# Attention stage of a macaron transformer block: weighing at steps 1, 5, 9 and 13, bank orders reversed between batches, a V projection two steps later, statistics one batch later

## The reference

```python
x = x + 0.5 * ffn(layernorm(x))     # x: (16, 256, 128) float32, 16 batches of 256 tokens
x = x + attn(layernorm(x))          # 16 heads of 8, softmax over 256 keys, biases
x = x + 0.5 * ffn(layernorm(x))
# ffn: silu(x W1) * (x W2) -> gelu(. H1) -> gelu(. H2) -> . W3, hidden width 512
```

## Time and profile before

| | us |
|---|---|
| median of 3 runs | 666.66 (664.96 to 670.3) |
| profiled execution | 672.58, its span 670.8 |
| attention stage, from the first `max_rows` to the first matmul of the second feed-forward phase | 225.12 to 490.85 |
| PE busy | 630.9 (94%) |
| ACT busy | 466.8 (70%) |
| DVE busy | 440.4 (66%) |

### The profile page before, as it was taken

The page is one execution under the profiler, slowest core; times in us unless marked ns, Lnnn a source line. Parts: engine busy times, 40 slices in busy tenths (PEclk is TensorE's granted clock), DMA queues, the critical chain, the costliest instruction groups (busy, mean ns, idle before and its releaser), DMA issues.

```text
span 670.8 us, 12974 instructions
## 1 busy us (share of the span) xinstructions
PE 630.9 (94%) x4452; PEld 462.1 (69%) x4452; DVE 440.4 (66%) x1036; ACT 466.8 (70%) x791; POOL 92.4 (14%) x256
## 2 busy tenths in 40 slices
PE   1969999999999799999999999999999999999996
PEld 1748878788776566666666566666567878878785
DVE  4844666858545867877878887784076485656742
ACT  2646786968864357777777868774477796887964
POOL 2601010012101012222222222102001001010000
PEclk9969999999999679999999999995689999999999
DMA  9100000000051704370715343300000001001011
GB/s 296 41 2 1 1 0 0 1 0 0 1 195 56 251 2 153 101 245 13 249 62 189 118 133 127 128 1 1 1 3 1 1 0 33 0 0 31 1 31 33
DMA packets 36674, 41.97 MB, mean 63 GB/s; under 512 B 2448, under 2 KB 27280, under 8 KB 36624
## 3 DMA queue, kind: packets, MB, share of 16 engines
q1 hardware_dynamic: 36624, 41.31, 18.2%
HBM read 22.42 MB, written 18.87 MB: 62 GB/s over the span
## 4 chain that ended last, share of the span: by engine, by line
PE 82%; DVE 7%; ACT 4%; issue 3%; DMA 2%; POOL 0%; SPq 0%; ACTq 0%; POOLq 0%
PE bank L1008 45%; PE bank L1118 10%; PE bank L1092 7%; PE bank L1105 5%; PE bank L1107 4%; DVE neg_max L816 2%; PE bank L1150 2%; PE bank L1136 2%; ACT probs L630 1%; PE bank L1081 1%; PE bank L1073 1%; PE bank L1055 1%; DVE act_lo L766 1%; PE bank L1077 1%; DMA QK<-qk_scratch 1%
## 5 line engine op out<-in xcount | busy, mean ns | idle before, releaser
L1008 PE MATMUL bank<-act_hi,WH 128*128 128x512 f32 x576 | 233.3, 405 | 6.8 <-issue 5.4
L1008 PE MATMUL bank<-act_lo,WH 128*128 128x512 f32 x576 | 228.8, 397 | 0.0
L816 DVE TENSOR_REDUCE neg_max<-bank 128x2 f32<-128x512 f32 x256 | 166.9, 682 | 50.0 <-PE bank L1092 46.8
L630 ACT ACTIVATE probs<-bank 128x512 f32<-128x512 f32 x256 | 140.8, 597 | 54.6 <-PE bank L1107 52.5
L786 DVE TENSOR_TENSOR act_lo<-full,act_hi 128x512 fp32r<-128x512 f32 x128 | 88.0, 689 | 124.2 <-ACT act_hi L529 124.1
L527 ACT ACTIVATE full<-bank,SG 128x512 f32<-128x512 f32 x128 | 88.0, 687 | 69.1 <-PE bank L1008 68.7
L1008 PEld LDWEIGHTS bank<-act_hi,WH 128*128 128x128 f32 x576 | 109.1, 189 | 37.2 <-issue 6.0
L1008 PEld LDWEIGHTS bank<-act_lo,WH 128*128 128x128 f32 x576 | 109.1, 189 | 25.4 <-issue 0.5
L1105 PE MATMUL bank<-QK 32*128 32x256 f32 x512 | 113.0, 348 | 3.5 <-ACT probs L630 1.8
L1107 PE MATMUL bank<-m_parts,SEL 32*128 32x256 f32 x512 | 96.0, 293 | 0.0
L1092 PE MATMUL bank<-QK 32*128 32x256 f32 x512 | 83.1, 340 | 6.7 <-DVE neg_max L816 4.8
(11 more groups left out here) (91 smaller groups left out, 597.2 us busy)
## 6 DMA issues: line engine op xcount, KB each, us to landing
qk_scratch<-qk SPq DMA_DIRECT2D x64, 256.0 KB, 2.6
QK<-qk_scratch SPq DMA_DIRECT2D x16, 1024.0 KB, 7.2
X<-x SPq DMA_DIRECT2D x4, 512.0 KB, 6.9
raw_rest<-w_ffn SPq DMA_DIRECT2D x4, 512.0 KB, 6.1
out<-X SPq DMA_DIRECT2D x4, 512.0 KB, 3.2
raw<-w_ffn SPq DMA_DIRECT2D x3, 256.0 KB, 4.4
WA<-w_att SPq DMA_DIRECT2D x1, 256.0 KB, 5.2
xT<-sel SPq DMA_DIRECT2D x1, 256.0 KB, 5.1
```

The costliest lines, as they stand in the source:

```text
L630: A.activation(probs[:, v % 8, :], bank[B_BANKS[v]][:, :], ACT.Exp, scale=SCALE)\
L816: D.tensor_reduce(neg_max[:, bb, qt, n0:n0 + 2], bank[banks[u]][:, :].rearrange("p (h k) -> p h k", h=2), axis=AX.X, op=ALU.max, negate=Tr ...
L1008: ins = MM(dst, a, b, start=k == 0, stop=k == len(todo) - 1)
```

## The change

- PE weighs where v % 4 == 1, from v = 5 on: behind steps 9 and 13 of the batch and steps 1 and 5 of the next one. `in_step` ends two units earlier, and ACT's `evacuate_o` moves from step 7 to step 5.
- Even batches take the banks in the order 0, 1, 5 (and 2, 3, 7), odd batches in the order 5, 1, 0 (and 7, 3, 2). Unit 0 finds its bank used two units back, unit 1 four back, every other unit three back.
- `project_v` and ACT's `set_v` move from step 7 to step 9. `transpose_att` stays at step 7, now with no weighing ahead of it.
- The statistics of the second feed-forward phase move from batch 14 (steps 7 to 11) to batch 15 (steps 2 to 6), its normalisation from step 3 to step 10 of batch 15; POOL takes `max_again` of batch 15 before the Newton steps.

```diff
-A_BANKS = (0, 1, 5) * 4 + (0, 1, 5, 1)
-B_BANKS = (2, 3, 7) * 4 + (2, 3, 7, 3)
+A_BANKS = ((0, 1, 5) * 5 + (0,), (5, 1, 0) * 5 + (5,))
+B_BANKS = ((2, 3, 7) * 5 + (2,), (7, 3, 2) * 5 + (7,))
...
-            return [(d, v) for d, v in at if 0 <= v < UNITS + 4]
+            return [(d, v) for d, v in at if 0 <= v < UNITS + 2]
+
+        def used_last(banks, prev, u):
+            before = prev + banks[:u]
+            return next((d for d in range(1, len(before) + 1) if before[-d] == banks[u]), u + 1)
...
+            max_again(NBATCH - 1, 1)
             rsqrt_steps(NORMS1, K * NORMS1)
-            max_again(NBATCH - 1, 1)
...
-                        if v == UNITS + 3:
+                        if v == UNITS + 1:
                             evacuate_o(b - d)
...
-                    if u == 7 and v_pair is not None:
+                    if u == 9 and v_pair is not None:
                         set_v(*v_pair)
...
-                elif not more:
-                    steps, norm = norm_steps(NORMS1, 0, biased=4), (NORMS1, 0, 8)
...
-                attend(2 * i + 1, 1, prev2=not first, more=more, norm=norm)
+                if more:
+                    attend(2 * i + 1, 1, prev2=not first, norm=norm)
+                else:
+                    attend(2 * i + 1, 1, more=False, steps=norm_steps(NORMS1, 0, biased=4), steps_at=2,
+                           norm=(NORMS1, 0, 8), norm_at=10)
...
-                ahead = next(d for d in range(1, UNITS) if banks[u - d] == banks[u])
-                wait(pe, max_done, UNITS * b + u - ahead + 1)
+                wait(pe, max_done, UNITS * b + u - used_last(banks, prev, u) + 1)
...
-                last = next(d for d in range(1, UNITS) if B_BANKS[v - d] == B_BANKS[v])
-                wait(pe, exp_done, UNITS * b + v - last + 1 + CREDIT)
+                wait(pe, exp_done, UNITS * b + v - used_last(B_BANKS[bb], B_BANKS[1 - bb], v) + 1 + CREDIT)
...
-                        if v >= 7 and v % 4 == 3:
+                        if v >= 5 and v % 4 == 1:
                             weigh(*at, v // 4 - 1, 0)
                             weigh(*at, v // 4 - 1, 1)
...
-                    if u == 7 and v_pair is not None:
+                    if u == 9 and v_pair is not None:
```

More of the change, by code:

```diff
@@ L624, in _, with exp_unit @@
             ffn_phase(0)
-            def exp_unit(b, v):
+            def exp_unit(b, bb, v):
                 act.wait_ge(b_mm, UNITS * b + v + 1)
                 act.wait_ge(pv_mm, GROUPS * b + v // 4 - 2 + 1 + CREDIT)
-                A.activation(probs[:, v % 8, :], bank[B_BANKS[v]][:, :], ACT.Exp, scale=SCALE)\
+                A.activation(probs[:, v % 8, :], bank[B_BANKS[bb][v]][:, :], ACT.Exp, scale=SCALE)\
                     .then_inc(exp_done, 1)
@@ L644, in o_to_sbuf, with attend @@
                 A.activation(onT[:, :], bank[6][:, 0:SEQ], ACT.Copy).then_inc(on_T_sb, 1)
-            def attend(b, prev=True, prev2=True, own=True, steps=UNITS, ahead=None, v_pair=None):
+            def attend(b, bb, prev=True, prev2=True, own=True, steps=UNITS, ahead=None, v_pair=None):
                 for u in range(steps):
@@ L651, in attend @@
                         if v < UNITS:
-                            exp_unit(b - d, v)
-                        if v == UNITS + 3:
+                            exp_unit(b - d, (bb + d) % 2, v)
+                        if v == UNITS + 1:
                             evacuate_o(b - d)
@@ L672, in att_body @@
             def att_body(i, par, ahead=True, more=True, first=False):
-                attend(2 * i, prev=not first, prev2=not first, v_pair=(i + 1, 1 - par) if more else None)
-                attend(2 * i + 1, prev2=not first, ahead=i + 2 if ahead else None)
+                attend(2 * i, 0, prev=not first, prev2=not first, v_pair=(i + 1, 1 - par) if more else None)
+                attend(2 * i + 1, 1, prev2=not first, ahead=i + 2 if ahead else None)
             att_body(0, 0, first=True)
@@ L682, in _ @@
             att_body(NPAIR - 1, 1, ahead=False, more=False)
-            attend(NBATCH, own=False, steps=SKEW + 4)
+            attend(NBATCH, 0, own=False, steps=SKEW + 4)
             ffn_phase(1)
@@ L810, in set_bias, with max_unit @@
                 D.tensor_tensor(BO[:, :], bank[3][:, 0:P], BO[:, :], op=ALU.add).then_inc(bias_set, 1)
-            def max_unit(b, bb, u, banks=A_BANKS):
+            def max_unit(b, bb, u, banks=None):
                 dve.wait_ge(a_mm, UNITS * b + u + 1)
@@ L816, in max_unit @@
                 D.tensor_reduce(neg_max[:, bb, qt, n0:n0 + 2],
-                                bank[banks[u]][:, :].rearrange("p (h k) -> p h k", h=2), axis=AX.X,
+                                bank[(banks or A_BANKS[bb])[u]][:, :].rearrange("p (h k) -> p h k", h=2), axis=AX.X,
                                 op=ALU.max, negate=True).then_inc(max_done, 1)
@@ L944, in _, with attend @@
             ffn_phase(0)
-            def attend(b, bb, prev=True, prev2=True, more=True, steps=(), norm=None):
+            def attend(b, bb, prev=True, prev2=True, more=True, steps=(), steps_at=7, norm=None, norm_at=3):
                 for u in range(UNITS):
@@ L956, in attend @@
                         add_att(b - 2, 2 * b - 4)
-                    if u == 3 and norm is not None:
+                    if u == norm_at and norm is not None:
                         n, tile0, width = norm
@@ L961, in attend @@
                             normalise(n, tile0 + 4, 4)
-                    if u >= 7:
-                        for step in steps[u - 7:u - 6]:
+                    if u >= steps_at:
+                        for step in steps[u - steps_at:u - steps_at + 1]:
                             step()
@@ L1083, in project_v, with max_scores @@
                 ins.then_inc(v_mm, 1)
-            def max_scores(b, par, bb, u, banks=A_BANKS):
+            def max_scores(b, par, bb, u, banks, prev):
                 qt, jj, lane = a_unit(u)
                 rows = slice(32 * lane, 32 * lane + 32)
-                ahead = next(d for d in range(1, UNITS) if banks[u - d] == banks[u])
-                wait(pe, max_done, UNITS * b + u - ahead + 1)
+                wait(pe, max_done, UNITS * b + u - used_last(banks, prev, u) + 1)
                 for i in range(2):
@@ L1100, in scores @@
                 rows = slice(32 * lane, 32 * lane + 32)
-                last = next(d for d in range(1, UNITS) if B_BANKS[v - d] == B_BANKS[v])
-                wait(pe, exp_done, UNITS * b + v - last + 1 + CREDIT)
+                wait(pe, exp_done, UNITS * b + v - used_last(B_BANKS[bb], B_BANKS[1 - bb], v) + 1 + CREDIT)
                 for i in range(2):
-                    dst = bank[B_BANKS[v]][:, SEQ * i:SEQ * i + SEQ]
+                    dst = bank[B_BANKS[bb][v]][:, SEQ * i:SEQ * i + SEQ]
                     MM(dst, k_of(2 * par + bb)[rows, 2 * jj + i, P * kt:P * kt + P],
@@ L1173, in entry @@
                                 pe.wait_ge(v_set, 1)
-                            max_scores(0, 0, 0, u, ENTRY_BANKS)
+                            max_scores(0, 0, 0, u, ENTRY_BANKS, ())
                     pe.wait_ge(h_full, hl + 6)
@@ L1292, in attend @@
                     if more:
-                        max_scores(b + 1, npar, nbb, u)
+                        max_scores(b + 1, npar, nbb, u, A_BANKS[nbb], A_BANKS[bb] if prev else ENTRY_BANKS)
                     for d, v in in_step(u, prev, own):
```

## The result

| | before | after |
|---|---|---|
| median, us | 666.68 (664.96 to 670.3) | 690.06 (688.19 to 693.0) |
| ratio | | 1.0347, interval 1.0285 to 1.041 |
| profiled span | 670.8 | 691.2 |
| PE / ACT / DVE busy | 630.9 / 466.8 / 440.4 | 621.2 / 463.9 / 438.8 |

The account below looks back on a forecast made before the run. PE was taken as the bound, waiting 4.1 us per pair of batches; +11.5 (batches 2 to 11), +2.7 (12, 13), -2.45 (14) and -3 (tail) made +8.8, with the profiled execution 5.9 above the median 675.4 us, range 662 to 692.

Parts of the forecast that it names:

- The sum: PE's waits laid out by hand, plus statistics and tail: 11.5 + 2.7 - 2.45 - 3 = +8.8 us.
- changes of kind: PE blocks following another kind, 0.23 us each: 14 in an even batch instead of 16, 18 in an odd instead of 19.
- The chart of an even batch: Hand layout of PE's blocks from max_rows to the next: 16.14 us, before 15.05, +1.09.
- The waits for exponentials: Even batch, steps 9 and 13: PE waits for ACT's exponentials 2 and 6, 0.76 us twice.
- the wait for `split_max`: PE stands ahead of transpose_o from 2.07 to 2.93 us in every batch, 0.86, no longer covered by a weighing.
- Odd batches: PE waits for split_max, for add_att ahead of transpose_att, and for scale_o: 17.08 us, before 15.96, +1.12.
- The clock within the stage: Rival: waits of about 1 us bring two more stretches at 1.2 GHz, 7 us each, 689; chance 0.2.
- Batch 14: Without the eight statistics it is as batch 13, 15.05 us against 17.50: -2.45, no clock fall at step 8.
- The tail: Batch 15 and the tail, 30.9 us before: gain between 0 and 10.4 depending on the clock, taken as -3.
- the tail stays fast: Rival: batch 15 and the tail at 2.4 GHz, all of the 10.4 us instead of 3, 668; chance 0.1.
- The bank orders and V: Steps 15 and 1 lose a short wait, step 0 gains one inside scale_o's; V at step 9 costs nothing.
- The rule on changes of kind: A change of tiling mode drains TensorE; by this alone eight pairs would be 5.5 us faster.

Follow-up runs that it names:

- e3: The changed kernel with DVE's split_max ahead of maximum 2 instead of behind it: 681.15 us, ratio 1.0321 to before.
- e1: The changed kernel with the weighing, and ACT's copy of o, put back behind steps 3, 7, 11 and 15: 640.9 us, ratio 0.9685 to before.
- e9: The changed kernel with the weighing of step 1 ahead of max_rows instead of behind it: 671.5 us, ratio 1.0081 to before.
- e4: The kernel before with the late statistics alone: 663.97 us, ratio 0.9979.
- e5: The changed kernel with PE repeating the first max_scores matmul at steps 1 and 3, and step 7 of odd batches: 689.15 us, ratio 1.0305 to before.
- e10: The kernel before with the reversed bank orders of odd batches alone: 662.98 us, ratio 0.9908.
- e6: e1 with the bank orders of before; V at step 9 and late statistics stay: 651.81 us, ratio 0.976 to before.
- e7: e1 with V back at step 7, right behind the weighing there: 650.08 us, ratio 0.9721 to before.
- e2: The kernel before with only the weighing moved, behind steps 1, 5, 9, 13, and ACT's copy of o at step 5: 699.74 us, ratio 1.0584.
- e11: e1 with DVE repeating maximum 2 twice and maximum 15 once into spare cells: 666.91 us, ratio 1.0006 to before.

## Why the prediction was right and wrong

**The direction and the mechanism were right; the size was not.** The sum said that the new order costs more waits than it saves changes of kind. The chart of an even batch came out block by block. With 0 at `max_rows` of batch 4 (293.46), forecast and measured: `transpose_o` 2.93 and 2.98, `project_out` 5.00 and 5.04, weighing 7.80 and 7.78, V 8.80 and 8.78, weighing 12.05 and 11.97, next `max_rows` 16.14 and 16.20. The waits for exponentials, 0.76 twice in this chart, are booked only in part (0.19 and 0.18, ahead of them, to DVE), but the weighings behind them start when forecast. e3 shows the wait for `split_max` by itself (0.49 of it can be taken back), e1 all the waits together.

**Odd batches: 0.54 too short.** Forecast 17.08, measured 17.62. Two terms failed. One is the latency of 0.04 from an engine's end to PE's start: `add_att` ends at 316.89 and `transpose_att` starts at 317.02, 0.13; `scale_o` ends at 327.14 and `max_rows` starts at 327.28, 0.14. The other is a wait of which the chart has nothing, K's 0.17 for ACT's `qk_full`. `transpose_att` starts at 7.36 instead of 7.20, K at 11.63 instead of 11.24. The two terms make 0.36 of the 0.54; the rest is small differences. Five odd batches: 2.7 us.

**The clock within the stage: the term that was missing, some 11 us.** By e9 it is 2.4 in batch 3, 1.4 in batch 13 and 7.5 in batch 14. The forecast had it as a rival, with 7 us for each fall and 689 for two of them, at a chance of 0.2. The time is 690; that the two are so near is in part luck, as there were three falls, of quite other sizes. It came on top of the forecast's order: e9, whose order is worth 6 us, takes 671.5 without falls before 487, so after without them would take about 677, its tail at 2.4 GHz included. That the forecast was 675.4 is near by luck: with a fast tail its terms give 668. Of the 9 us between, 2.7 are the odd batches and 5.9 are what was taken off because before's profiled execution lay above its median; e9's lies at its median. The argument against the rival was that each wait is short and between dense blocks. This is the step that failed: the clock fell behind waits of 0.61 and 0.41, 1.2 us apart, which the sum had put into one place. The fall of before had been put down to its one wait of 1.39 alone.

**The falls against those of before.** Behind the stage's entrance, the low clock costs after little more than it cost before. The fall that the statistics bring about cost 12.4 us in batch 14 and the tail (e4 against before), and the change does away with it; the forecast had 5.45 for that. The new falls cost 16. So most of the 20.4 are waits at 2.4 GHz, some 14 of them in batches 2 to 11 (16.7 less the 2.4 of batch 3).

**Batch 14: -2.45 forecast, +5.0 measured.** That the statistics leave it was worth more than forecast (e4: -3.83 with the old weighing), and e5, which has the order of after and no fall there, takes 15.04 (forecast 15.05). What failed is the step "batch 14 is as batch 13, no fall at its step 8": there is none at step 8, there is one 0.9 us into the batch, behind the two waits at its start, and the batch takes 7.9 more than in e9.

**The tail: -3 forecast, -4.5 measured.** Low for its first 9 us, then at 2.4 GHz. The forecast leaned to the low end since the earlier trace rows had a fall at 482. e1 (21.0), e9 (21.7) and e4 (22.3) show that the tail holds 2.4 GHz but for its last 5 us at most when no fall stands ahead of it. So the rival "the tail stays fast" was underrated at 0.1, and its 20.5 was near. That -3 came out near -4.5 is luck: the low 9 us come from the fall in batch 14, which the forecast had ruled out.

**The bank orders and V: their gain was in the sum, but not seen.** The prediction said that the reversed orders' gain at steps 15 and 1 exists and that V at step 9 costs nothing. With the old weighing they are worth 1.6 to 1.7 and 0.67 per pair (e10, e6, e7). With the new weighing both together win 0.65 (34.45 against 33.80), since PE waits for `scale_o` in any case and what is won ahead is waited for there. A chart of the change's parts without the weighing, which the same durations allow, might have shown it; none was made.

**The rule on changes of kind** (the Trainium skill, TensorEngine Tiling (Array Packing), Key Properties). By it alone the kernel would have been faster; the sum of the waits decided. PE's busy time fell from 630.9 to 621.2 at nearly the same mean clock, but busy time overlaps, and no run here measures a change of kind by itself.

## What to carry to other kernels

A long block that waits for nothing is worth most right behind the steps that feed another engine and ahead of the block that needs the answer: before such a block is moved, list which waits it covers now, and count them as costs of the move. When a change is a bundle, lay out the order by hand once without its largest part; here three of the four parts were good for 25 us and the fourth cost 49. And price such waits twice: for their length, and for the chance that PE's clock falls behind them, as it did in three batches of after.

## What was not expected of the hardware

**Waits of half a microsecond to one can be enough for the clock.** In the middle of the stage no wait was over 1.02 us in after or in any experiment, and the clock fell in after, e2, e3, e5 and e11. Ahead of after's three falls stand 0.61 at step 0 and 0.40 or 0.41 at `max_rows`, ahead of e3's the same or 0.51 and 0.3, ahead of e2's one wait of 1.00 or 1.02, ahead of e11's in the middle 0.6 and 0.9, and ahead of e5's 0.5 to 0.6 and a fill. But waits of the same length also passed. In after 0.61 and 0.41 did so at the start of batch 2, 0.60 and 0.40 at that of batch 12, and 0.52 and 0.3 at all eight of batches 4 to 11; in e2 a wait of 1.0 stands ahead of each of thirteen batches, and the clock fell behind two. e9 has the waits of after at step 0 and ahead of `transpose_o`, but none ahead of `max_rows`, and its clock holds; e5 has a fill in that last place, and its clock does not. What decides between two such places is open, and what the fill of e5 lacked as well.

**The entrance varies, and V may have a part in it.** At the stage's entrance the clock comes back at 235 in e1 and e9, 237 in after, 244 in before, 253 in e7 and e10 and 258 in e4; batches 0 and 1 take 6.8 us more in e7 than in e1. In all eight kernels with V at step 9 it comes back between 234 and 238, in four of the five with V at step 7 between 244 and 258 (e2, with the new weighing, at 236). Batch 0 has a V block too, so the edit does act there, and the 1.9 us that after wins in batches 0 and 1 may be its work. With one trace for each kernel this is not shown. Batch lengths of the steady middle are the better measure of an edit there.

**The second feed-forward phase starts late.** `add_att` of the last batch ends at 505.96 and the phase's first matmul starts at 509.97, 4.0 us later; in before it is 486.92 and 490.85, 3.9, though there PE had weighings and transposes to do in between and here nothing but the transposes. Timeline of after:

```profile
505.54 0.42 DVE L858 TENSOR_TENSOR X<-bank,X 128x256 f32<-128x256 f32 x1 [5.25 <-PE bank L1156]
...
506.02 1.09 PE L1063 MATMUL bank<-EYE,xn 128*128 128x128 f32 x8 [0.52 <-DVE X L858]
...
509.97 0.77 PE L1016 MATMUL bank<-x_hi,WH 128*128 128x512 f32 x1 [2.85 <-issue]
```

2.85 us stand as issue, although DVE's x_lo, from 507.40 on, is through at 508.7. In e1 and e3 the same gap, 2.28 and 2.39, is booked to x_lo, which in e1 too is through 0.7 us before PE starts (456.9 and 457.63). It was not tried what fills the gap.
